# An attention stage on one core: output product in three float32r passes, the mask as the exponential's bias, the reciprocals in another place

## The reference

```python
# x (8, 512, 256), ctx_1024 (8, 512, 256), mask (8, 512) bool
lat = layernorm(layernorm(x)) * gl + bl          # 512 queries of a batch element
f   = layernorm(ctx_1024) * gm + bm              # 512 context keys
kv  = concat([f, lat], axis=1)                   # 1024 keys; only the first 512 can be masked
q = heads(lat @ Wq) * 64 ** -0.5                 # 16 heads of 64
k = heads(kv @ Wk); v = heads(kv @ Wv)
sim = q @ k.T
sim = sim - max(sim)
sim = where(kv_mask, sim, -inf)
out = softmax(sim) @ v
x = x + merge(out) @ Wo                          # Wo (1024, 256)
```

## Time and profile before

| | us |
|---|---|
| median of 3 runs | 3542.01 |
| lowest and highest of them | 3534.15, 3543.56 |
| the profiled execution's own time | 3545.15 |
| its span, first to last instruction | 3543.5 |
| PE busy in the span | 3194.5 (90%) |
| DVE busy | 2050.7 (58%) |
| ACT busy | 1269.2 (36%) |
| POOL busy | 1648.1 (47%) |

### The profile page before, as it was taken

The page is one execution under the profiler, slowest core; times in us unless marked ns, Lnnn a source line. Parts: engine busy times, 40 slices in busy tenths (PEclk is TensorE's granted clock), DMA queues, the critical chain, the costliest instruction groups (busy, mean ns, idle before and its releaser), DMA issues. The chain is left out here.

```text
span 3543.5 us, 56164 instructions
## 1 busy us (share of the span) xinstructions
PE 3194.5 (90%) x17981; PEld 2291.4 (65%) x17982; DVE 2050.7 (58%) x4462; ACT 1269.2 (36%) x1778; POOL 1648.1 (47%) x945
## 2 busy tenths in 40 slices
PE   4885999999639999999999999999999966699988
PEld 4555888888525666666666666666666555577766
DVE  5666455555645666666766667666666653122235
ACT  2232333333234444444444444444444432122222
POOL 5202333333234665666656666556665545500037
PEclk8995999999859999999999999999999958899999
DMA  5100000000161010110101101011010031322223
GB/s 145 72 0 1 21 11 13 9 13 9 66 248 43 31 68 31 64 45 30 69 28 67 45 30 68 27 68 45 30 68 28 7 106 59 130 79 63 62 69 110
DMA packets 89978, 192.94 MB, mean 54 GB/s; under 512 B 12768, under 2 KB 58152, under 8 KB 83760
## 3 DMA queue, kind: packets, MB, share of 16 engines
q1 hardware_dynamic: 74288, 155.99, 12.6%
q0 software_dynamic: 11392, 27.36, 2.5%
q10 hardware_dynamic: 4224, 8.65, 0.7%
HBM read 137.60 MB, written 54.30 MB: 54 GB/s over the span
## 5 line engine op out<-in xcount | busy, mean ns | idle before, releaser
L2037 POOL TENSOR_TENSOR d_acc<-d_acc,d_pr 128x1024 f32<-128x1024 f32 x384 | 938.6, 2444 | 91.6 <-ACT d_pr L1941 60.5
L1941 ACT ACTIVATE d_pr<-d_p 128x1024 f32<-128x1024 f32 x512 | 488.2, 1026 | 237.4 <-PE d_p L1876 237.2
L1810 PE MATMUL d_pO<-d_pr,d_V 128*64 128x512 f32 x2048 | 473.1, 599 | 0.0
L2037 POOL TENSOR_TENSOR d_acc<-d_pr 128x1024 f32<-128x1024 f32 x64 | 153.0, 2391 | 623.1 <-ACT d_pr L1941 623.1
L1986 DVE TENSOR_REDUCE d_nm<-d_p 128x2 f32<-128x1024 f32 x256 | 304.6, 1222 | 95.0 <-PE d_p L1853 95.0
L1981 DVE CUSTOM_DVE_ANT_0 d_biased<-d_p,d_masked 128x512 f32<-128x512 f32 x512 | 330.6, 688 | 31.5 <-issue 31.5
L946 POOL TENSOR_TENSOR e_hs<-e_hf,e_hs 128x512 fp32r<-128x512 f32 x136 | 175.9, 1293 | 364.8 <-ACT e_hs L923 364.8
L1810 PEld LDWEIGHTS d_pO<-d_pr,d_V 128*64 128x64 f32 x2048 | 135.4, 136 | 261.8 <-issue 223.3
L976 DVE SCALAR_TENSOR_TENSOR res<-e_pY,m_Wt,res 128x256 f32<-128x256 f32 x544 | 225.8, 477 | 45.7 <-PE e_pY L884 44.9
L1997 DVE RECIPROCAL d_rb<-d_rb 128x128 f32<-128x128 f32 x256 | 224.6, 920 | 9.3 <-ACT d_rb L1934 9.3
L884 PEld LDWEIGHTS e_pY<-e_Wd,e_hs 128*128 128x128 f32 x1632 | 213.5, 191 | 13.8 <-POOL e_hs L946 2.2
(11 more groups left out here) (288 smaller groups left out, 5659.6 us busy)
## 6 DMA issues: line engine op xcount, KB each, us to landing
d_W<-w_split SPq DMA_DIRECT2D x32, 1536.0 KB, 6.4
kv_split<-c_ys SPq DMA_DIRECT2D x16, 1024.0 KB, 6.1
d_kv<-kv_split SPq DMA_DIRECT2D x8, 2048.0 KB
d_masked<-mask_bias SPq DMA_DIRECT2D x64, 256.0 KB
x_slots<-m_zeros SPq DMA_DIRECT2D x1, 9088.0 KB, 29.8
b_x<-x_slots SPq DMA_DIRECT2D x71, 128.0 KB
y_slots<-b_y SPq DMA_DIRECT2D x71, 128.0 KB
w_split<-a_wqs POOLq DMA_DIRECT2D x4, 1536.0 KB, 5.5
```

The source lines that it names most:

```text
L1810: last = pe.matmul(pO[own[h], :], V[vb][:, s, par * P + h * HD1:par * P + (h + 1) * HD1], pr[:, s % PT, h, :], start=(s == 0), stop=(s == ...
L1941: act.activation(pr[:, n % PT, :, :], slot(st, what, n)[:, :, :], ACT.Exp).then_inc(exp_done, 1)
L2037: pool.tensor_tensor(acc[:, q, :, :], a, pr[:, s % PT, :, :], ALU.add).then_inc(acc_done, 1)
```

## The change

Three things are changed in the `d_` phase.

1. The output product becomes three float32r passes. `OT` is single now; ACT copies it to a high part (new unit `oh`), DVE subtracts (new unit `ol`), both into `OS`. `Wo` is split once at the start, after landing in the second values tile. `YY` has 12 matmuls and waits for `ol`.
2. The mask is no longer a row of the keys' matrix. `KM` goes, with its DMAs; a constant `first_row` takes its place in the first of the four terms. The mask is a `[128, 1]` column, the bias operand of the exponential. The columns of all batch elements are gathered in the first phase by one DMA (`mask_col`, 128x64 single elements); in each step DVE copies eight of them to `key_bias`, ahead of `N`.
3. In even steps the reciprocals move: `r0` ahead of `S4`, and `r1` to `r3` and the product `OT` ahead of `S5`. In odd steps they stay; `oh` comes ahead of `S3` and `ol` behind it.

```diff
+                    sp.wait_ge(m_out, 16)
+                    sp.dma_start(io["mask_col"][:, :], io["mask_bias"].rearrange("b (s p) -> p (b s)", p=P),
+                                 allow_slow_non_contiguous=True).then_inc(col_in, 16)
+                    sp.wait_ge(col_in, 16)
...
-    """M KK Q ST0 ST1 ST2 S0 S1 PV0 PV1 S2 ST3 S3 den PV2 PV3 S4 ST4 r0 ST5 r1 r2 ST6 ST7 S5 PV4 r3 PV5 PV6 PV7 O
-       S6 S7 YY N""".split(),
-    """Q KK M VV0 den S0 ST0 ST1 S1 ST2 ST3 ST4 ST5 ST6 r0 ST7 r1 r2 S2 r3 PV0 PV1 PV2 PV3 S3 S4 S5 PV4 PV5 PV6 PV7
-       S6 S7 VV1 N O YY""".split())
+    """M KK Q ST0 ST1 ST2 S0 S1 PV0 PV1 S2 ST3 S3 den PV2 PV3 r0 S4 ST4 r1 ST5 r2 r3 ST6 ST7 oh S5 ol PV4 PV5
+       PV6 PV7 O S6 S7 YY N""".split(),
+    """Q KK M VV0 den S0 ST0 ST1 S1 ST2 ST3 ST4 ST5 ST6 r0 ST7 r1 r2 S2 r3 PV0 PV1 PV2 PV3 oh S3 ol S4 S5 PV4 PV5
+       PV6 PV7 S6 S7 VV1 N O YY""".split())
...
-        KH, KL, KM = ([sb(f"d_{n}{j}", [P, KEYS], F32R) for j in range(2)] for n in ("KH", "KL", "KM"))
+        KH, KL = ([sb(f"d_{n}{j}", [P, KEYS], F32R) for j in range(2)] for n in ("KH", "KL"))
+        first_row = sb("d_first_row", [P, P], F32R)
...
-        OT = sb("d_OT", [P, 2, S])
-        Wo = sb("d_Wo", [P, NPAIR, D])
+        OT = sb("d_OT", [P, S])
+        OS = sb("d_OS", [P, 2, S], F32R)
+        Wo = sb("d_Wo", [P, NPAIR, 2, D], F32R)
...
-                sp.wait_ge(set_up, SET_UP)
-                for j in range(2):
-                    for h in range(2):
-                        sp.dma_start(KM[j][h * HD1:h * HD1 + 1, :].bitcast(F32), onerow[:, :].bitcast(F32)
-                                     ).then_inc(set_rows, 16)
-                sp.wait_ge(set_rows, 4 * 16)
+                sp.dma_start(V[1][:, :, :], io["wo1"]).then_inc(wo_in, 16)
                 sp.dma_start(W[1][:, :, :, :, :].bitcast(F32), wsp[1]).then_inc(w_in[1], 16)
-                sp.dma_start(Wo[:, :, :], io["wo1"]).then_inc(wo_in, 16)
...
-                        if not first and not (isinstance(st.g, int) and st.g == 0):
-                            sp.wait_ge(st_done, NKT * st.g)
-                        for h in range(2):
-                            sp.dma_start(KM[j][h * HD1 + 1:h * HD1 + 2, :].bitcast(F32),
-                                         mb[bass.ds(bb, 1), :]).then_inc(mask_in[j], 16)
...
-                            terms = [(KM[q], QM), (KL[q], QH[q]), (KH[q], QL[q]), (KH[q], QH[q])]
+                            keys = slice(s * P, (s + 1) * P)
+                            terms = [(first_row[:, :], QM), (KL[q][:, keys], QH[q]), (KH[q][:, keys], QL[q]),
+                                     (KH[q][:, keys], QH[q])]
                             for i, (k_, q_) in enumerate(terms):
                                 for h in range(2):
-                                    last = pe.matmul(out[:, h, :], k_[own[h], s * P:(s + 1) * P],
+                                    last = pe.matmul(out[:, h, :], k_[own[h], :],
                                                      q_[own[h], :], start=(i == 0), stop=(i == len(terms) - 1))
...
-                            pe.wait_ge(ot_done, st.g + 2)
+                            if isinstance(st.g, int) and st.g == 1:
+                                pe.wait_ge(wo_lo, 1)
+                            pe.wait_ge(ot_lo, st.g)
                             out = slot_free(what)
-                            wo = Wo[:, bass.ds(4 * st.batch_half + st.off - 1, 1), :].rearrange("p a d -> p (a d)")
+                            wo = Wo[:, bass.ds(4 * st.batch_half + st.off - 1, 1), :, :].rearrange(
+                                "p a w d -> p (a w) d")
                             for t in range(TPB):
-                                last = pe.matmul(out[:, t // 2, (t % 2) * D:(t % 2 + 1) * D],
-                                                 OT[:, 1 - q, t * P:(t + 1) * P], wo, start=True, stop=True)
+                                for n_, (op, wp) in enumerate(PASSES):
+                                    last = pe.matmul(out[:, t // 2, (t % 2) * D:(t % 2 + 1) * D],
+                                                     OS[:, op, t * P:(t + 1) * P], wo[:, wp, :],
+                                                     start=(n_ == 0), stop=(n_ == len(PASSES) - 1))
                             last.then_inc(y_done, 1)
                 for_steps(pe, emit)
...
+                act.wait_ge(wo_in, 16)
+                act.copy(Wo[:, :, HI, :], V[1][:, :, :]).then_inc(wo_hi, 1)
+                act.wait_ge(wo_lo, 1)
...
+                        if what == "oh":
+                            act.wait_ge(ot_done, st.g + 2)
+                            act.copy(OS[:, HI, :], OT[:, :]).then_inc(ot_hi, 1)
...
+                            if n == 0:
+                                act.wait_ge(bias_ready, st.g + 1)
...
-                            act.activation(pr[:, n % PT, :, :], slot(st, what, n)[:, :, :], ACT.Exp
-                                           ).then_inc(exp_done, 1)
+                            act.activation(pr[:, n % PT, :, :], slot(st, what, n)[:, :, :], ACT.Exp,
+                                           bias=key_bias[:, q, n:n + 1]).then_inc(exp_done, 1)
...
+                dve.wait_ge(wo_hi, 1)
+                dve.tensor_tensor(Wo[:, :, LO, :], V[1][:, :, :], Wo[:, :, HI, :].bitcast(F32),
+                                  ALU.subtract).then_inc(wo_lo, 1)
...
+                        if what == "ol":
+                            dve.wait_ge(ot_hi, st.g)
+                            dve.tensor_tensor(OS[:, LO, :], OT[:, :], OS[:, HI, :].bitcast(F32), ALU.subtract
+                                              ).then_inc(ot_lo, 1)
...
+                            if first or st.off == 0:
+                                bb = 0
+                            else:
+                                bb = st.b + st.batch_half if st.off >= 3 else st.b
+                            dve.tensor_copy(key_bias[:, j, :], mask_col[:, bass.ds(NKT * bb, NKT)]
+                                            ).then_inc(bias_ready, 1)
...
-                                dve.tensor_tensor(OT[:, 1 - q, :], osb[:, 1 - q, :], rb[:, :], ALU.mult
+                                dve.tensor_tensor(OT[:, :], osb[:, 1 - q, :], rb[:, :], ALU.mult
```

More of the change, by code:

```diff
@@ L269, in layer0_attention @@
                  "y_done y_added biased").split())
-            wr_in, m_in, m_ready, wq_hi, wq_lo, wq_out, m_out = (sem2("a_" + n) for n in (
-                "wr_in m_in m_ready wq_hi wq_lo wq_out m_out").split())
+            wr_in, m_in, m_ready, wq_hi, wq_lo, wq_out, m_out, col_in = (sem2("a_" + n) for n in (
+                "wr_in m_in m_ready wq_hi wq_lo wq_out m_out col_in").split())
             def known(b, *values):
@@ L1570, in present @@
         return kind in ("Q", "KK", "VV", "S", "N")
-    if kind in ("den", "r", "YY"):
+    if kind in ("den", "r", "oh", "ol", "YY"):
         return st.g > 0
@@ L1650, in for_steps, with layer1_pairs @@
     emit(Step(NSTEP, 0, NSTEP // 2, B - 1, 1, 4))
-def layer1_pairs(nc, io, res, ident, kv_d, wsp, mb):
+def layer1_pairs(nc, io, res, ident, kv_d, wsp, mb, mask_col):
     with ExitStack() as ctx:
@@ L1678, in layer1_pairs @@
         ones = sb("d_ones", [P, HD1])
-        onerow = sb("d_onerow", [1, KEYS], F32R)
+        key_bias = sb("d_key_bias", [P, 2, NKT])
         ahead = sb("d_ahead", [P, 8])
@@ L1694, in layer1_pairs @@
         MAXES = 3 * TPB + 1
-        SET_UP = 8
+        SET_UP = 6
         def maxes_before(n):
@@ L1856, in emit @@
                         elif what == "M":
-                            if isinstance(st.g, int) and st.g == 0:
-                                pe.wait_ge(wo_in, 16)
-                                pe.wait_ge(set_rows, 4 * 16)
                             bank(what)
@@ L1953, in _ @@
                 dve.memset(ahead[:, 5:6], 0.0).then_inc(y_added, 1)
+                dve.wait_ge(wo_hi, 1)
+                dve.tensor_tensor(Wo[:, :, LO, :], V[1][:, :, :], Wo[:, :, HI, :].bitcast(F32),
+                                  ALU.subtract).then_inc(wo_lo, 1)
                 def emit(st):
                     j, gp, by2 = pair(st)
+                    first = isinstance(st.g, int) and st.g == -1
                     q = st.parity
                     for what, n in order(st):
-                        if what == "KK":
+                        if what == "ol":
+                            dve.wait_ge(ot_hi, st.g)
+                            dve.tensor_tensor(OS[:, LO, :], OT[:, :], OS[:, HI, :].bitcast(F32), ALU.subtract
+                                              ).then_inc(ot_lo, 1)
+                        elif what == "KK":
                             dve.wait_ge(k_hi, gp + 1)
@@ L1972, in emit @@
                             if n == 0:
-                                dve.wait_ge(mask_in[j], 48 * by2 + 48)
+                                dve.wait_ge(mask_in[j], 16 * by2 + 16)
                             if m == 0:
@@ L2010, in _ @@
```

(14 more changed lines are left out.)

9 lines of the change are left out of this document (4 added, 5 removed).

## The result

The changed kernel takes 3609.11 us (median of 4 runs, 3606.51 to 3611.57). The kernel before, run beside it, takes 3538.08 us. The ratio is 1.0201, 95% interval 1.0182 to 1.0220: slower by 2.0%. The profiled execution took 3606.51 us, its span is 3604.9 us.

The account below looks back on a forecast made before the run. PE was taken as the bound. Per pair 2.0 + 0.26 + 0.03 - 0.15 = 2.14 us, 66.3 over 31 pairs, plus 1.4: +68 on 3545.15, 3613, less 3.1: 3610 us; whole range 3548 to 3626.

Parts of the forecast that it names:

- the sum: All predicted terms for the whole kernel: 2.14 us per pair, 66.3 over 31 pairs, plus 1.4 at the end: +68 us.
- The tie: Odd step: DVE's low-part subtraction starts behind POOL's add and waits; PE then stalls before S7 and VV1, 2.0 us.
- rival of a won tie: Odd step: subtraction goes ahead of POOL's add, no stall there, M waits 0.3 us; 15 us, 3557 us; chance 0.18.
- float32r product: Output product on PE: 12 matmuls at 0.124 us take 1.49 us, saving 0.15 us in a pair.
- rival "faster product": Output product on PE: 12 matmuls at 0.107 us, 1.28 us, rest hidden; saves 0.62 per pair, 3524 us; chance 0.07.
- Bias column: Exponentials on ACT: 0.086 us longer each, making PE wait 0.26 us in a pair.
- the two places: Where PE waits for an exponential: ST2 in odd steps, 0.09 us, S1 in even steps, twice 0.086; together 0.26.
- Low part, even step: DVE's subtraction waits for POOL's add, ends near when the output product wants to start: 0 to 0.1 us, 0.03 taken.
- Tail: Last output product, without cover: high and low part come on the path, matmuls about 0.1 less: +1.4 us.
- Hidden parts: KM's DMAs, mask gather, splitting Wo once, high part on ACT: each taken as 0 us.
- Mask copy: DVE, ahead of N: one more small instruction, 0.1 to 0.2 us, or the rest of a POOL add.

Follow-up runs that it names:

- e1: Changed kernel, but DVE writes the product into a PSUM bank instead of the SBUF tile OT, and high and low part read it there: 3534.05 us.
- e2: Changed kernel with the unit ol behind S5 instead of behind S3 in the odd step's list: 3548.45 us.
- e11: Kernel before with only the change's float32r output product (in an SBUF tile) and moved reciprocals, the mask as before: 3617.52 us, ratio 1.0223.
- e8: Changed kernel with a single-column POOL addition put between the fourth and fifth add of an odd step: 3599.42 us.
- e5: Changed kernel with six unread matmuls in each odd step, four between S6 and S7, two between S7 and VV1: 3600.4 us.
- e4: Kernel before with only the float32r output product and moved reciprocals, the product in a PSUM bank, the mask as before: 3527.25 us.
- e3: Changed kernel with the exponential's bias operand left out, the mask column copy and all waits kept: 3607.59 us.

## Why the prediction was right, step by step

3610 us were predicted, 3609.11 measured. The phase grew by 73.3 us where the sum had 68, and the terms agree less well than the sum. Measured terms are differences of PE's group costs (start to next start), summed over the rhythm.

- **The tie (decides).** Predicted lost, with 1.2 us ahead of `S7` and 0.8 ahead of `VV1`. Measured 1.54 - 0.33 = 1.21 and 1.13 - 0.33 = 0.80. It was lost in 28 pairs, not 31: 56 us instead of 62. e1, e2 and e11 show the cause. Taking it as lost was a choice by the nearest row, and a close one: in e8 the side changed within some 0.01 us. The rival of a won tie describes the last three pairs, its 0.3 us at `M` included (measured 0.39).
- **The clock was missing.** No step of the prediction asked what PE's pause would do to the granted clock. 9 falls of 1.49 us: 13 us. e5 shows that the pauses make them. The trace of before has the sign of it, in the last step of the phase: PE's timeline with a pause ahead of `M`, and the windows view (its clock is the 0.50) right behind.

```profile
2824.75 0.63 PE L1863 MATMUL d_pm<-d_identr,d_nm 128*128 128x128 f32 x4 [2.35 <-DVE d_nm L1991]
2825.42:2832.25 6.83, 6.19 (x24) 3.65 (x26) 3.51 (x5) 2.65 (x4) 0.00 (x0) 0.50 0.00 0
```

- **The float32r product was mis-sized:** 0.15 us in a pair, measured 0.60 in e4. The step that failed took a float32 group to cost nothing behind the next group's start. The group behind the old product took 0.19 us longer than behind the new one. That made -5 us of what is -17. The rival "faster product" had nearly this size (0.62), but not this mechanism: it wanted 1.28 us from `YY` to the next group in an odd step, and that is 1.43.
- **Bias column:** 0.26 in a pair, measured 0.35 (11 us): at the two places as predicted (0.18 at `S1`, 0.09 at `ST2`), and another 0.08 over the rest of the odd step's exponentials. The duration, 0.086 predicted, is 0.091.
- **Low part, even step:** 0.03, measured 0.22 (7 us); without the bias column it is 0.15 (e11). That it ends just where `YY` could start was right; that `YY` then starts 0.26 us late was not counted. e1 shows this term to be the same lock.
- **Tail:** +1.4 predicted, 8.17 - 6.80 = 1.37 from `den` to `YY` measured. **Hidden parts** (`KM`'s DMAs, the mask gather, the split of `Wo`, the high part): none shows on PE. **Mask copy:** it took over `N`'s wait, as the one or the other was bound to.

Together 56 + 13 + 11 + 7 - 17 + 1.4 = 71 us, and the 2 us that are left of the phase's 73 lie in its first and last steps. The errors of the product (12 too dear) and of the three pairs (6) covered the missing clock (13), the even step (6) and the column (3). The right number came with a right mechanism, but part of it by luck. The other phases were 12 us shorter in the profiled execution of after than in that of before, which is why its span grew by 61 us only.

Open: why the clock falls in 9 of 28 stalled steps in one kernel and in 18 or 19 in others with the same stall. The falls are not scattered: in the changed kernel they come two or three pairs apart, in e3 and e11, whose pairs are shorter, one or two. What picks the steps these runs do not show.
